# Where two small batched products run in a two-layer graph network kernel: in two stretches of each step, or in one

## The reference

```python
x = layernorm(x + (adj*adj).T @ x + bias)                 # layer 0
zl = x @ W_lang.T;  zg = x @ W_grav.T;  v = x @ W_V.T     # layer 1
A_l = max(cosine(zl, zl), 0) * (1 - eye)
A_g = exp(-max(squared_distance(zg), 0) / (2 * sigma**2)) * (1 - eye)
K = w * row_normalised(A_l * adj) + (1 - w) * row_normalised(A_g * adj)
x = layernorm(x + (K @ v) @ W_O.T)
```

## Time and profile before

| what | value |
|---|---|
| median of three executions | 611.86 us |
| the profiled execution, its own time | 611.51 us |
| its span, first to last instruction | 609.7 us |
| TensorE matmul busy | 592.6 us (97%) |
| TensorE weight load busy | 456.2 us (75%) |
| VectorE busy | 365.6 us (60%) |
| ScalarE busy | 299.6 us (49%) |
| GpSimd busy | 131.3 us (22%) |
| mean granted TensorE clock | 0.994 |

### The profile page before, as it was taken

How to read it: one execution, slowest core, us unless ns; L and a number is a source line. 1 busy time by engine, 2 the same in 40 slices (tenths; PEclk the granted TensorE clock), 3 DMA queues, 4 the chain that set the end, 5 groups by cost and what they waited for, 6 DMA issues and landing times.

```text
span 609.7 us, 10056 instructions
## 1 busy us (share of the span) xinstructions
PE 592.6 (97%) x3803; PEld 456.2 (75%) x3803; DVE 365.6 (60%) x814; ACT 299.6 (49%) x532; POOL 131.3 (22%) x344
## 2 busy tenths in 40 slices
PE   7999999999999999999999999999999999999992
PEld 6787868778686877778686877868687777868771
DVE  3854365657747575665746564774757566574366
ACT  2654435455363636445464545536363644546413
POOL 0201102122220311222130212222031122213022
PEclk9999999999999999999999999999999999999997
DMA  7901104040311304031220403031130400101003
GB/s 239 263 2 43 27 1 104 34 105 35 70 53 45 78 35 104 36 69 70 58 65 19 103 35 104 36 70 53 43 79 37 104 34 1 70 1 53 17 18 121
DMA packets 20703, 38.68 MB, mean 63 GB/s; under 512 B 2096, under 2 KB 2096, under 8 KB 20656
## 3 DMA queue, kind: packets, MB, share of 16 engines
q1 hardware_dynamic: 20656, 38.05, 21.6%
HBM read 21.27 MB, written 16.78 MB: 62 GB/s over the span
## 4 chain that ended last, share of the span: by engine, by line
PE 93%; DMA 3%; DVE 1%; SPq 1%; ACT 1%; issue 0%; POOL 0%; POOLq 0%
PE ring L335 65%; PE bank_s L350 10%; PE bank_y L295 5%; PE bank_z L393 5%; PE bank_y L310 3%; DMA h_sb<-in_L_gnn_W_V_dram 3%; PE bank_z L310 2%; PE ring L437 2%; PE bank_s L359 1%; PE bank_s L376 1%; PE bank_y L369 1%; SPq L237 0%; DVE hT_lo L829 0%; ACT hT_hi L498 0%; DVE h_sb L763 0%
## 5 line engine op out<-in xcount | busy, mean ns | idle before, releaser
L335 PE MATMUL ring<-hT_hi,T_hi 128*128 128x512 f32 x320 | 131.0, 409 | 0.0
L335 PE MATMUL ring<-hT_hi,T_lo 128*128 128x512 f32 x320 | 125.2, 391 | 0.0
L498 ACT ACTIVATE yT<-ring 128x512 f32<-128x512 f32 x128 | 74.6, 597 | 98.0 <-PE ring L335 98.0
L335 PE MATMUL ring<-hT_lo,T_hi 128*128 128x512 f32 x288 | 112.4, 390 | 0.0
L335 PE MATMUL ring<-M_hi,hT_hi 128*128 128x512 f32 x256 | 103.2, 403 | 0.0
L335 PE MATMUL ring<-M_hi,hT_lo 128*128 128x512 f32 x256 | 100.3, 392 | 0.0
L335 PE MATMUL ring<-M_lo,hT_hi 128*128 128x512 f32 x256 | 99.6, 389 | 0.0
L335 PEld LDWEIGHTS ring<-hT_hi,T_hi 128*128 128x128 f32 x320 | 60.0, 188 | 35.0 <-ACT yT L498 13.0
L498 ACT ACTIVATE u_sb<-ring 128x512 f32<-128x512 f32 x64 | 38.0, 597 | 82.7 <-PE ring L335 82.7
L666 DVE TENSOR_TENSOR h_sb<-bank_y,bias_bc 128x512 f32<-128x512 f32 x64 | 42.4, 686 | 52.8 <-PE bank_y L295 52.7
L335 PEld LDWEIGHTS ring<-hT_hi,T_lo 128*128 128x128 f32 x320 | 60.1, 188 | 13.3
(11 more groups left out here) (103 smaller groups left out, 838.5 us busy)
## 6 DMA issues: line engine op xcount, KB each, us to landing
out_dram<-h_sb SPq DMA_DIRECT2D x64, 256.0 KB, 2.0
x_sb<-in_x_dram SPq DMA_DIRECT2D x30, 512.0 KB, 6.4
x_sb<-in_x_dram SPq DMA_DIRECT2D x4, 256.0 KB, 5.4
yT<-in_L_gnn_W_lang_dram SPq DMA_DIRECT2D x1, 1024.0 KB, 5.8
yT<-in_L_gnn_W_grav_dram SPq DMA_DIRECT2D x1, 1024.0 KB, 9.5
h_sb<-in_L_gnn_W_O_dram SPq DMA_DIRECT2D x1, 1024.0 KB, 11.7
h_sb<-in_L_gnn_W_V_dram SPq DMA_DIRECT2D x1, 1024.0 KB, 15.4
bias_bc<-in_L_gnn_bias_dram SPq DMA_DIRECT2D x1, 256.0 KB, 6.3
```

What stands on the lines that cost most here:

```text
L335: last = pe.matmul(ring[ring_of(k)][:, :], a, b, start=n == 0, stop=n == len(terms) - 1)
L498: return act.activation(dst, src, ACT.Copy, scale=scale)
```

## The change

`layer0` half 1 moves up beside half 0, and `apply_k` half 1 beside its half 0: after projection 2 and `transpose_k` TensorE runs four calls in a row. For that each call gets banks of its own: `layer0` half 1 writes `bank_s` and one tile of the ring, `apply_k` half 1 writes `bank_y`. The ring's tile is taken in turn as if it were a projection between 2 and 3 (`place`, `AT_Y`), so TensorE's waits for a free ring tile are counted anew (`ring_free`). `layer0` half 1 now waits for `copy_kt` (it writes over `kt_ps` in `bank_s`) and for the ring tile; `apply_k` half 1 waits for the first two `add_y`; `gram` also waits for the third `add_y`, projection 5 for the fourth. Transposes 0 and 1 both stand ahead of `gram`, and wait for all four `add_z`. In the last group `transpose_k(g-1)` moves behind projection 5 and `rows` waits for three `add_z`.

Helpers and TensorE:

```diff
-    def ring_of(k):
-
-        return (NSETUP + k) % NRING
+
+    AT_Y = 3
+
+    def place(g, k):
+
+        return (NPROJ + 1) * g + k + (g < NG - 1 and k >= AT_Y)
+
+    def ring_of(g, k):
+
+        return (NSETUP + place(g, k)) % NRING
+
+    def ring_of_y(g):
+
+        return (NSETUP + (NPROJ + 1) * (g - 1) + AT_Y) % NRING
...
+        def y_bank(g, p):
+            if p < 2:
+                return bank_y[p]
+            if g == 0:
+                return bank_z[p - 2]
+            return bank_s if p == 2 else ring[ring_of_y(g)]
+
+        def z_bank(p):
+
+            return bank_z[p] if p < 2 else bank_y[p - 2]
...
+            def ring_free(n):
+
+                g = min((n - NRING) // (NPROJ + 1), NG - 1)
+                k = n - NRING - (NPROJ + 1) * g
+                if g < NG - 1 and k == AT_Y:
+                    pe.wait_ge(y_added, NP * g + 2 * NP)
+                else:
+                    pe.wait_ge(proj_out, NPROJ * g + k - (g < NG - 1 and k > AT_Y) + 1)
+
...
             def layer0(g, h):
...
                 if h:
-                    pe.wait_ge(y_added, NP * g + 2)
+                    if g > 1:
+                        pe.wait_ge(kt_copied, g - 1)
+                    if g > 0:
+                        ring_free((NPROJ + 1) * (g - 1) + AT_Y)
                 elif g > 0:
...
-                        last = pe.matmul(bank_y[a][half(c), :], mix[half(a), :], x_sb[g % 2][half(a), 2 * h + c, :],
+                        last = pe.matmul(y_bank(g, 2 * h + a)[half(c), :], mix[half(a), :], x_sb[g % 2][half(a), 2 * h + c, :],
...
             def transpose_h(g, p):
                 pe.wait_ge(h_ready, NP * g + p + 1)
-                if p < 2:
-                    pe.wait_ge(y_added, NP * g + NP)
-                elif g > 1:
-                    pe.wait_ge(z_added, NP * g - NP)
-                elif g == 1:
+                if g > 1:
+                    pe.wait_ge(z_added, NP * g - 2 * NP + (2 if p > 1 else NP))
+                elif g == 1 and p > 1:
                     pe.wait_ge(hT_split, p + 1)
                     pe.wait_ge(hT_copied, p + 1)
...
             def project(g, k):
...
-                    pe.wait_ge(proj_out, NPROJ * g + k - NRING + 1)
+                    ring_free(place(g, k))
...
             def gram(g):
...
                     pe.wait_ge(kt_copied, g)
+                if g < NG - 1:
+                    pe.wait_ge(y_added, NP * g + NP + 3)
...
             def rows(g):
...
+                else:
+                    pe.wait_ge(z_added, NP * g - 1)
...
             def apply_k(g, h):
                 pe.wait_ge(kt_copied, g + 1)
                 pe.wait_ge(proj_out, NPROJ * g + 2 * DC + 2 * h + 2)
-                if h:
-                    pe.wait_ge(z_added, NP * g + 2)
-                elif g < NG - 1:
+                if g == NG - 1:
+                    pe.wait_ge(z_added, NP * g)
+                    pe.wait_ge(x0_done, g + 1)
+                elif h and g < NG - 2:
+                    pe.wait_ge(y_added, NP * g + 2 * NP + 2)
+                else:
                     pe.wait_ge(hT_split, NP * g + 2 * NP)
                     pe.wait_ge(hT_copied, NP * g + 2 * NP)
-                else:
-                    pe.wait_ge(z_added, NP * g)
+                    if h:
+                        pe.wait_ge(x0_done, g + 1)
...
-                        last = pe.matmul(bank_z[a][half(c), :], KT[half(a), h, half(c)], u_sb[half(a), 2 * h + c, :],
+                        last = pe.matmul(z_bank(2 * h + a)[half(c), :], KT[half(a), h, half(c)], u_sb[half(a), 2 * h + c, :],
...
             def step(g, tail=True):
...
                 if tail:
                     transpose_k(g - 1)
                 layer0(g + 1, 0)
+                layer0(g + 1, 1)
                 if tail:
                     apply_k(g - 1, 0)
+                    apply_k(g - 1, 1)
                 project(g, 3)
                 project(g, 4)
                 project(g, 5)
-                layer0(g + 1, 1)
-                if tail:
-                    apply_k(g - 1, 1)
                 project(g, 6)
-                transpose_h(g + 1, 0)
                 project(g, 7)
                 project(g, 8)
+                transpose_h(g + 1, 0)
+                transpose_h(g + 1, 1)
                 gram(g)
-                transpose_h(g + 1, 1)
                 project(g, 9)
                 transpose_h(g + 1, 2)
                 transpose_p(g)
...
             g = NG - 1
             project(g, 0)
             project(g, 1)
             project(g, 2)
-            transpose_k(g - 1)
             project(g, 3)
             project(g, 4)
             project(g, 5)
+            transpose_k(g - 1)
             project(g, 6)
             project(g, 7)
             apply_k(g - 1, 0)
```

ScalarE (`evict` uses `ring_of(g, k)`):

```diff
         def _(act):
             def step(g, tail=True):
...
                 evict(g, 3)
                 evict(g, 4)
                 normalise_h(g + 1, 0)
+                normalise_h(g + 1, 1)
                 evict(g, 5)
-                normalise_h(g + 1, 1)
-                hi_hT(g + 1, 0)
+                if tail:
+                    normalise_out(g - 1, 0)
                 evict(g, 6)
-                copy_hT(g + 1, 0)
                 evict(g, 7)
                 evict(g, 8)
-                if tail:
-                    normalise_out(g - 1, 0)
-                    normalise_out(g - 1, 1)
+                copy_p(g)
+                hi_hT(g + 1, 0)
                 normalise_h(g + 1, 2)
                 normalise_h(g + 1, 3)
-                copy_p(g)
-                copy_hT(g + 1, 1)
+                copy_hT(g + 1, 0)
                 hi_hT(g + 1, 1)
                 evict(g, 9)
+                hi_hT(g + 1, 2)
+                copy_hT(g + 1, 1)
+                copy_hT(g + 1, 2)
+                if tail:
+                    normalise_out(g - 1, 1)
+                evict(g, 10)
+                hi_hT(g + 1, 3)
+                copy_hT(g + 1, 3)
+                exp_g(g)
                 if tail:
                     normalise_out(g - 1, 2)
-                copy_hT(g + 1, 2)
-                hi_hT(g + 1, 2)
-                hi_hT(g + 1, 3)
-                evict(g, 10)
-                copy_hT(g + 1, 3)
                 evict(g, 11)
                 if tail:
                     normalise_out(g - 1, 3)
-                exp_g(g)

...
             g = NG - 1
             evict(g, 0)
-            copy_kt(g - 1)
             evict(g, 1)
             evict(g, 2)
             evict(g, 3)
+            copy_kt(g - 1)
             evict(g, 4)
             evict(g, 5)
             evict(g, 6)
             evict(g, 7)
             copy_p(g)
+            exp_g(g)
             normalise_out(g - 1, 0)
             evict(g, 8)
             evict(g, 9)
-            exp_g(g)
+            evict(g, 10)
+            normalise_out(g - 1, 1)
             copy_kt(g)
-            normalise_out(g - 1, 1)
-            evict(g, 10)
             evict(g, 11)
             normalise_out(g - 1, 2)
             normalise_out(g - 1, 3)
```

VectorE (`add_y` reads `y_bank(g, p)`, `add_z` reads `z_bank(p)`):

```diff
         def _(dve):
             def step(g, tail=True):
                 add_y(g + 1, 0)
                 add_y(g + 1, 1)
+                add_y(g + 1, 2)
+                count_y(g + 1, 0)
                 if tail:
                     add_z(g - 1, 0)
-                count_y(g + 1, 0)
+                add_y(g + 1, 3)
+                if tail:
+                    add_z(g - 1, 1)
+                count_y(g + 1, 1)
                 if tail:
                     count_z(g - 1, 0)
-                    add_z(g - 1, 1)
-                add_y(g + 1, 2)
-                if tail:
                     add_z(g - 1, 2)
-                add_y(g + 1, 3)
-                if tail:
                     count_z(g - 1, 1)
                     gather_z(g - 1, 0)
+                    add_z(g - 1, 3)
+                diagonals(g)
+                shift(g)
+                if tail:
                     count_z(g - 1, 2)
-                count_y(g + 1, 1)
-                if tail:
-                    add_z(g - 1, 3)
                     count_z(g - 1, 3)
-                diagonals(g)
                 lo_hT(g + 1, 0)
-                shift(g)
                 if tail:
                     gather_z(g - 1, 1)
                 lo_hT(g + 1, 1)
...
             g = NG - 1
             add_z(g - 1, 0)
             add_z(g - 1, 1)
-            diagonals(g)
-            shift(g)
             count_z(g - 1, 0)
             count_z(g - 1, 1)
             gather_z(g - 1, 0)
+            diagonals(g)
+            shift(g)
             add_z(g - 1, 2)
+            count_z(g - 1, 2)
             add_p(g)
+            add_z(g - 1, 3)
             weigh(g)
             coefficients(g)
             combine(g)
-            add_z(g - 1, 3)
-            count_z(g - 1, 2)
             count_z(g - 1, 3)
             gather_z(g - 1, 1)
             add_z(g, 0)
...
             count_z(g, 1)
             add_z(g, 2)
             gather_z(g, 0)
+            add_z(g, 3)
```

(9 more changed lines are left out.)

## The result

The changed kernel takes 605.97 us (median of four executions, 605.54 to 606.21) against 611.87 for the kernel before (611.76 to 613.67) beside it; the measured ratio is 0.9888, with a 95% interval from 0.9862 to 0.9914 (the two medians alone give 0.9904). The interval is wide because executions of the kernel before scatter. Forecast were 606.8 us and 0.8%.

What follows compares the result with a forecast made beforehand. TensorE, busy throughout a step, bounds the kernel; -5.25 (merge) + 0.45 (transposes) - 0.25 (end) = -5.05 us from 611.51 gives 606.5, plus 0.35 for the median 606.8 us. Own range 605.4 to 608.4; 8 in 10 reaches up to 610.0.

Steps and rivals of the forecast that it cites:

- What bounds the kernel: TensorE, busy 34.85 of 34.85 us in a step at full clock; only a shorter stream of matmuls shortens the step.
- One stretch instead of two: Steps 0 to 14: one entrance and exit of the 64 by 64 tile shape goes, 0.35 us each, 5.25 us gained.
- the bounds 0.14 and 0.40: Lowest and highest gain per step allowed for merging the stretches, 2.1 and 6.0 us in all.
- Transpose 1 ahead of `gram`: Around gram: moving the transpose costs between -0.06 and +0.10 us a step; +0.03 taken, 0.45 us lost.
- New waits: Walk through one step's queues for new waits of TensorE: each place has margin or cover, costed at nothing.
- the tightest place: Next step's projection 0 waiting for lo_hT 3: 0.1 to 0.3 us to spare, costed at nothing.
- The end: Last group: apply_k half 1 no longer waits for two add_z; 0.25 us gained, bounds 0 and 0.5.
- The setup: Setup before the steps runs through the same banks as before; costed at nothing.
- The sum: Whole kernel: -5.25 + 0.45 - 0.25 = -5.05 us, giving 606.8 us, 0.8% faster.
- The rivals: Four alternative outcomes, two of them named below, with chances 0.09, 0.07, 0.08 and 0.06 against 0.70 for the forecast.
- A: Projection 0 waits for tile 3's late low part, 0.1 to 0.25 us a step; 609.8 us; chance 0.09.
- C: rows on TensorE waits for inv_rep because GpSimd's columns comes late; slower, 619 us; chance 0.08.

Runs made afterwards that it cites:

- stretch_alone: Changed kernel with the merged stretch kept but transpose 0 back behind projection 6 and transpose 1 behind gram; 606.28 us, ratio 0.9907.
- tile_matmuls_more: Changed kernel plus two unused float32 matmuls in 64 by 64 tiles after projection 6; 615.75 us, one execution.
- transposes_alone: Kernel before, two stretches kept, with transposes 0 and 1 both ahead of gram and ScalarE's order as in the changed kernel; 612.49 us, ratio 1.0003.
- one_transpose_more: Changed kernel plus one unused transpose of the identity after projection 6 in each step; 608.40 us, one execution.
- late_low_part: Changed kernel with normalise_out 2 put ahead of the two copies of transpose 3 on ScalarE; 613.00 us, one execution.
- rows_joined: Changed kernel with rows moved behind transpose 3, GpSimd's columns ahead of z 1 and transpose 1 back behind gram; 611.52 us, ratio 0.9989.
- rows_joined_3: rows_joined with GpSimd's copy into inv_rep ahead of sq_eps and VectorE's lo_hT 0 behind gather_z 1; 604.91 us, ratio 0.9878.

## Why the prediction was right or wrong

- **What bounds the kernel**: right. TensorE is as full after as before, and the gain is its shorter stream.
- **One stretch instead of two**: right. Taken 0.35 a step, measured 0.346 in `stretch_alone`; the bounds 0.14 and 0.40 were not needed. The prediction also had an estimate of 0.11 for the pair from a page (the Trainium skill, TensorE: Matmul & The Clock Gate, "Step-by-step: what each phase is for"). It was right to go by the row: `tile_matmuls_more` has 0.29 to 0.34.
- **Transpose 1 ahead of `gram`**: the step that failed. The prediction put it as "I take +0.03, 15 x 0.03 = 0.45 us lost". `transposes_alone` measured -0.013, and beside the merged stretch it is 34.492 - 34.500 = -0.008: 0.1 to 0.2 us gained. The edges came out as forecast (0.04 for 0.03; 0.33 for the interval after `gram`). What was left out, put at nothing without a reason, is that the projections then have one run less, and that a run's start costs more than its first interval: 0.05 us here, spread over some ten intervals that each look like rounding. That an interruption has such a cost without a change of shape is shown by `one_transpose_more`; that it varies (0.02 to 0.06 in the runs here) goes with how many slow intervals follow, and why is open. The range of the term, -0.06 to +0.10, holds the measured value, but by luck: its lower bound was read from the edges alone. The value chosen in it was on the wrong side.
- **New waits**: right, TensorE was idle at none of the places that were walked through. The margins came out at 0.30 for projection 0 (0.1 to 0.3 forecast) and 1.0 for `rows` (0.7), and `apply_k` half 1 starts after 0.86, without loss. `late_low_part` shows that the tightest place was the right one.
- **The end**: 0.25 taken, 0.33 measured, for the right cause: `apply_k` half 1 starts at 592.30, 0.91 after half 0, where it had waited for `add_z`.
- **The setup**: costed at nothing. The profiles can't tell it from nothing: one of the kernel before has its end at 44.43, three of the changed kernel at 44.17 to 46.02, a scatter larger than the two terms above.
- **The sum**: -5.05 forecast, -5.65 from steps and end, near -6 between the medians. 0.6 of the difference is the transposes' term, 0.1 the end. The range was cut too close below: 605.4 is 611.86 - 6.0 - 0.5, with the transposes at nothing. By "below it nothing has a mechanism" it allowed the stretch its upper bound and left the transposes' lower bound, 0.06 x 15 = 0.9 us, out. (The upper end of the forecast's own range, 608.4, is 608.3 by its terms.) The first ratio of 0.9888 is 605.0 us for the 611.87 beside it, outside; the medians, 605.97 to 606.50, and the repetitions' 0.9900 and 0.9907, 605.8 and 606.2, are inside. Of the 1.8 us between 606.8 and 605.0, 0.6 are the transposes' term and some 1.0 is a first ratio lower than the repetitions found.
- **The rivals**: none came. A's and C's places are real (`late_low_part`, `rows_joined`), and both were given their price by this kernel's margins.

## What to carry to other kernels

On a full TensorE, count the places where the tile shape changes and those where a run of equal matmuls is interrupted, and price each by start-to-start intervals on both sides of it, not by busy time; work of one odd shape belongs in one stretch, and the price of the banks for it is extra waits that have to be walked through queue by queue. Then look at the margin in front of each wait: here 0.3 us was enough, and one operation more in the wrong queue took 0.5 us a step. Where a term's bounds lie on both sides of zero, carry both into the range.

## What was not expected of the hardware

- A run of projections (128 by 128 by 512, split float32) has intervals of 0.226 to 0.227 us in its middle and of 0.231 on the average over the first 2 to 10 after an interruption, even a single transpose of 0.11 us. They follow one fixed row, entered at different places. They add 0.01 to 0.06 us to a run. The cause is open.
- GpSimd's copy of 128 by 256 elements took 0.78 us when a VectorE subtraction with both operands in SBUF had begun 0.16 us before it, and 0.40 alone or when the copy began first; then the subtraction took 0.72 to 0.79 for 0.68. GpSimd's 4-column `sq_eps` took 0.59 (`rows_joined`) in place of 0.24. The Trainium skill has the rule (SBUF — State Buffer, "Who interferes with whom"): a VectorE instruction with two SBUF inputs contends with a GpSimd instruction that reads SBUF. The trace agrees, and `rows_joined_3` shows that moving the one instruction is enough.
